# Moving one subtraction of DVE behind two maxima in a cross-attention and expert kernel

## The chip, the cores and the metric

The kernel runs on one core of a Trainium2 chip. The metric is the device time of one execution in microseconds (us). Engines are named as the profile names them: PE is TensorE's matmul, PEld its weight load, DVE is VectorE, ACT is ScalarE, POOL is GpSimd, SP issues DMAs.

## The reference

`x` has 16 batches of 224 tokens of width 512, the context 16 batches of 750 rows of width 384. All is float32.

```python
def _L0_xattn_ref(x, context, Wq, bq, Wk, bk, Wv, bv, Wo, bo):
    q = x @ Wq.T + bq
    k = context @ Wk.T + bk
    v = context @ Wv.T + bv
    ...                                   # 16 heads of 32
    attn = jnp.einsum('bihd,bjhd->bhij', q, k) * SCALE
    attn = jax.nn.softmax(attn, axis=-1)
    out = jnp.einsum('bhij,bjhd->bihd', attn, v)
    out = out.reshape(B, NQ, IN_DIM)
    return out @ Wo.T + bo
...
x = x + _L0_xattn_ref(_layernorm(x, axis=-1), ctx_768, ...)
x = x + _L0_ffn_ref(_layernorm(x, axis=-1), ...)   # 8 experts 512-256-512, GELU, top 2 by router logits
```

The router's logits of a token are its cosine with each expert's centroid plus its product with the expert's routing weights.

## The kernel before

The first four fifths of the time are attention, the last fifth the experts. Attention works on 64 groups `g`, four heads each, so a batch `b` has four groups, `t = g % 4`. Each engine has an order written out by hand: four functions `first`, `second`, `third` and `fourth`, one per group of a batch, called with `(g, g // 4)` for `g` from 0 to 68. Below, a "quarter" is one such call. The engines meet only through counting semaphores.

In the quarter of group `g`, TensorE computes the scores, exponentials' products with the values and denominators around group `g`, while it also makes the maxima's scores for group `g + 1` and the projected keys of group `g + 2` (`K0`, `K1`: the first 376 and the last 374 of them). Projections are made in float32 accuracy from two parts: ScalarE writes the high part of an operand (a rounded float32), and DVE the low part, which is the value less the high part. TensorE multiplies high by high, high by low and low by high (`split3`, lines 388 to 390).

- `maximum(g, m)`, DVE, m = 0 to 5: the row maxima of the scores of group `g`. TensorE writes those scores (`score_for_max`, line 1823) in three rounds, each into banks 0 to 3, and the next round, or another unit in one of these banks, waits until they have been reduced.
- `k_lo(g, i)`, DVE: the low part of the keys, after ScalarE's `k_hi`; it frees the bank of `K0` or `K1`.
- `o_lo(g)`, DVE, line 1291: the low part `oT_l` of the turned (transposed) and normalised outputs of group `g`. Both its inputs, `o_s` and `oT_h`, are in SBUF, as is its output. It waits for ScalarE's `o_hi(g)`. TensorE's `project_o` of the second quarter needs it for all four groups of a batch, and ScalarE's `o_copy` of the next group waits for it before it overwrites `o_s`.
- `keep_logits(b, qt)`, DVE, lines 1369 and 1371: copies the router logits of a batch from PSUM and adds the cosines. TensorE's `turn_logits` (line 1757) makes them. The second call frees the logits' bank.
- `add_step(g, i)`, POOL, lines 631 and 634: adds up exponentials of 125 x 896 columns for the denominators, five steps per group. In the first quarter `add_bo` (line 650) stands ahead of steps 1 to 4; it waits for the load of the residual `x_res`.

PSUM banks of the array `M` are handed out by a fixed plan (`bank_plan`). Around the boundary between the first and the second quarter bank 4 goes, in this order, to `lg` (the logits), `K0` of the second quarter and `xT0`. `K1` of the second quarter goes to bank 1. A unit in bank 1 waits for the last round of maxima scores that was planned ahead of it, here `maximum(g + 1, 2)` of the second quarter.

On TensorE the second quarter begins with `score_for_max(g + 1, 0)`, two scores, `project_k(g + 2, 0)` (K0), two scores, `score_for_max(g + 1, 1)`, `values(g - 1, 2)`, `transpose_x(b + 1, 0)`, two scores, `project_k(g + 2, 1)` (K1).

Of the kernel before, what the change touches and what calls it, by code (L numbers as in the profile page):

```python
# [12 lines left out]
B, NQ, D = 16, 224, 512  # L13
# [133 lines left out]
def expert_phase(nc, x1_d, w1, b1, w2, b2, centroids, w_route, ident_d, gates_dram, out):  # L147
    x, ctxT, wqT, bq, wkT, bk, wvT, bv, woT, bo, ident, x1 = SCRATCH["attention"]
    with ExitStack() as es:
# [209 lines left out]
        def bank_of(kind, n):  # L359
            return M[:, UNITS[kind, n][0], :]  # L360
# [9 lines left out]
        def freed(kind, n):  # L370
            return misc_free[UNITS[kind, n][0]]
# [28 lines left out]
        with nc.Block() as block:  # L400
# [794 lines left out]
            def _(dve):  # L1195
# [28 lines left out]
                def xT_rest(b, i):  # L1224
                    if b >= B:
                        return
                    dve.wait_ge(xT_hi, 2 * b + i + 1)
                    dve.tensor_tensor(out=xT_l[:, 2 * i:2 * i + 2, :],
                                      in0=bank_of(f"xT{i}", b)[:, 0:2 * NQ].rearrange("p (c n) -> p c n", c=2),
                                      in1=xT_h[:, 2 * i:2 * i + 2, :], op=ALU.subtract).then_inc(freed(f"xT{i}", b), 1)  # L1230

                def q_lo(g):
                    if g >= GROUPS:
                        return
                    dve.wait_ge(qh_done, g + 1)
                    dve.scalar_tensor_tensor(out=ql_s[:, g % 2, :], in0=bank_of("Q", g)[:, 0:NQ],
                                             scalar=bq_s[:, g % NG:g % NG + 1], in1=qh_s[:, g % 2, :], op0=ALU.add,
                                             op1=ALU.subtract).then_inc(freed("Q", g), 1)

                def k_lo(g, i):  # L1240
                    if g >= GROUPS:
                        return
                    off, w = KHALF[i]
                    dve.wait_ge(kh_done, 2 * g + i + 1)
                    dve.scalar_tensor_tensor(out=kl_s[:, g % 2, off:off + w], in0=bank_of(f"K{i}", g)[:, 0:w],  # L1245
                                             scalar=bk_s[:, g % NG:g % NG + 1], in1=kh_s[:, g % 2, off:off + w],
                                             op0=ALU.add, op1=ALU.subtract).then_inc(freed(f"K{i}", g), 1)

                def maximum(g, m):
                    if not 0 <= g < GROUPS:  # L1250
                        return
                    u, pair = m // 2, slice(m % 2 * 2, m % 2 * 2 + 2)
                    if m == 0 and g:
                        dve.wait_ge(top_done, g)
                    dve.wait_ge(x_full, XU * g + u + 1)
                    if u < QT:
                        dve.tensor_reduce(mx_parts[0:QP, pair, u, 0:1], M[0:QP, pair, 0:FIRST_KEYS], AX.X,  # L1257
                                          ALU.max).then_inc(max_done, 1)
                        return
                    both = M[0:QP, pair, 0:QT * OTHER_KEYS].rearrange("p j (q n) -> p j q n", q=QT)  # L1260
                    dve.tensor_reduce(mx_parts[0:QP, pair, :, 1], both, AX.X, ALU.max).then_inc(max_done, 1)  # L1261

                def top(g):
                    if not 0 <= g < GROUPS:
                        return
                    if g:
                        wait_full(dve, "mT", g - 1)
                    dve.wait_ge(max_done, 2 * XU * (g + 1))
                    dve.tensor_reduce(mx[0:QP, :], mx_parts[0:QP].rearrange("p j q k -> p (j q) k"), AX.X,
                                      ALU.max).then_inc(top_done, 1)  # L1270

                def invert(g):
                    if not 0 <= g < GROUPS:
                        return
                    wait_full(dve, "den", g)
                    den = bank_of("den", g)[:, 0:NQ]
                    dve.reciprocal(den, den).then_inc(inverted, 1)  # L1277

                def normalise(g):
                    if not 0 <= g < GROUPS:  # L1280
                        return
                    dve.wait_ge(inverted, g + 1)
                    dve.wait_ge(ocopy_done, g + 1)
                    dve.tensor_tensor(out=o_s[:, :], in0=o_s[:, :], in1=bank_of("den", g)[:, 0:NQ],
                                      op=ALU.mult).then_inc(freed("den", g), 1)

                def o_lo(g):
                    if not 0 <= g < GROUPS:
                        return
                    dve.wait_ge(oh_done, g + 1)  # L1290
                    dve.scalar_tensor_tensor(out=oT_l[:, g % OS, :], in0=o_s[:, :], scalar=bv_s[:, g % NG:g % NG + 1],
                                             in1=oT_h[:, g % OS, :], op0=ALU.add, op1=ALU.subtract).then_inc(ol_done, 1)

                def residual(b, qt):
                    if not 0 <= b < B:
                        return
                    wait_full(dve, f"O{qt}", b)
                    dve.wait_ge(bo_added, QT * b + qt + 1)
                    x = residual_of(b)[0:QP, qt, :]
                    dve.tensor_tensor(out=x, in0=bank_of(f"O{qt}", b)[0:QP, :], in1=x,  # L1300
                                      op=ALU.add).then_inc(freed(f"O{qt}", b), 1)
# [17 lines left out]
                def y_stats_half(b, qt):  # L1319
                    if b:  # L1320
                        dve.wait_ge(newton2, roots(b))
                    wait_free(dve, f"O{qt}", b)
                    dve.bn_stats(stats2[0:QP, qt, :], residual_of(b)[0:QP, qt, :]).then_inc(y_stat, 1)
# [35 lines left out]
                def keep_logits(b, qt):  # L1359
                    if not 0 <= b < B:  # L1360
                        return
                    if b == B - 1:
                        last_logits(qt)
                        return
                    wait_full(dve, "lg", b)
                    dve.wait_ge(newton2, roots(b + 1))
                    both = logits_of(b, qt)
                    kept = lgs[0:QP, QT * b + qt, :]
                    dve.tensor_copy(kept, both[:, E:2 * E]).then_inc(lg_copied, 1)
                    dve.wait_ge(lg_copied, 3 * b + 2 * qt + 1)  # L1370
                    dve.scalar_tensor_tensor(out=kept, in0=both[:, 0:E], scalar=length[0:QP, qt:qt + 1], in1=kept,  # L1371
                                             op0=ALU.mult, op1=ALU.add).then_inc(freed("lg", b) if qt else lg_copied, 1)
# [24 lines left out]
                def w_part(n):  # L1397
                    src, hi, lo = pieces[n]
                    dve.wait_ge(ew_hi, n + 1)
                    dve.tensor_tensor(out=lo, in0=lo.bitcast(F32), in1=hi, op=ALU.subtract).then_inc(ew_lo, 1)  # L1400
# [14 lines left out]
                def first(g, b):  # L1415
                    maximum(g + 1, 0)
                    maximum(g + 1, 1)
                    k_lo(g + 2, 0)
                    q_lo(g + 2)
                    maximum(g + 1, 2)  # L1420
                    invert(g - 1)
                    maximum(g + 1, 3)
                    normalise(g - 1)
                    k_lo(g + 2, 1)
                    maximum(g + 1, 4)
                    maximum(g + 1, 5)
                    top(g + 1)
                    q_lo(g + 3)
                    o_lo(g - 1)
                    keep_logits(b - 2, 0)  # L1430
                    keep_logits(b - 2, 1)

                def second(g, b):
                    maximum(g + 1, 0)
                    maximum(g + 1, 1)
                    k_lo(g + 2, 0)
                    maximum(g + 1, 2)
                    xT_rest(b + 1, 0)
                    maximum(g + 1, 3)
                    invert(g - 1)  # L1440
                    k_lo(g + 2, 1)
                    normalise(g - 1)
                    residual(b - 1, 0)
                    if b == B:
                        y_stats_half(B - 1, 0)
                        w_part(4)
                    maximum(g + 1, 4)
                    maximum(g + 1, 5)
                    xT_rest(b + 1, 1)
                    top(g + 1)  # L1450
                    residual(b - 1, 1)
# [755 lines left out]
```

## Time and profile before

| | |
|---|---|
| median of three timed runs | 1476.07 us (1475.44 to 1480.64) |
| the profiled execution | 1481.48 us |
| its span in the profile | 1479.7 us |
| TensorE busy | 1393.8 us, 94% |
| POOL busy | 1078.5 us, 73% |
| DVE busy | 987.6 us, 67% |
| ScalarE busy | 840.7 us, 57% |

The span is what the profiler's records cover; the profiled execution's own time is 1.8 us more. Busy shares are averages over stages; which engine sets the time at a place is read from what waits for what there. Records of one engine can overlap by some 0.09 us, and an instruction's record can hold time in which it is held up. The rows that are used stand in their own section below.

### The profile page before, as it was taken

Reading aid. Unit: us, or ns where it says so; the run is one execution under the profiler, and the core shown is the slowest. Engines: PE = TensorE matmul, PEld = TensorE weight load, DVE = VectorE, ACT = ScalarE, POOL = GpSimd, SP = SyncE. Lnnn points to the kernel's source line nnn. Section 1 sums busy time; section 2 is a strip of 40 time slices with the busy share of each in tenths; the row PEclk is TensorE's granted clock in tenths of the full one; section 3 lists DMA queues with packets and bytes.
Section 4 is the critical chain, followed back from the end, with each engine's and each line's share of the span. In section 5 each row is a group of like instructions: output and inputs, shape, how many; then the busy total and the mean of one; then the engine's idle time right before and its main releaser. Section 6 shows DMA issues by size and latency. Waiting matters only on the chain.

```text
span 1479.7 us, 34315 instructions
## 1 busy us (share of the span) xinstructions
PE 1393.8 (94%) x11524; PEld 1110.1 (75%) x11524; DVE 987.6 (67%) x1429; ACT 840.7 (57%) x1825; POOL 1078.5 (73%) x915
## 2 busy tenths in 40 slices
PE   4899999999999999999999999999998777999997
PEld 4677777777777777778777777777786446888896
DVE  6666777767676767777777776767667485444443
ACT  4556655556656565666665555555564553555554
POOL 3468787877787878787877878777877814666765
PEclk9989999999999999999999999999999687999999
DMA  7354555555455554555555454545444753777775
GB/s 244 89 133 109 160 141 141 148 131 147 125 154 138 146 139 133 141 142 140 152 138 165 122 161 130 145 131 149 113 132 125 235 130 83 141 139 131 143 140 83
DMA packets 134952, 206.74 MB, mean 140 GB/s; under 512 B 33808, under 2 KB 70832, under 8 KB 134656
## 3 DMA queue, kind: packets, MB, share of 16 engines
q1 hardware_dynamic: 120544, 173.20, 43.2%
q0 software_dynamic: 14240, 31.35, 11.9%
q8 instruction: 99, 1.62, 0.5%
q14 instruction: 69, 0.57, 0.1%
HBM read 64.29 MB, written 38.66 MB: 70 GB/s over the span
## 4 chain that ended last, share of the span: by engine, by line
PE 83%; DVE 8%; SPq 3%; issue 2%; DMA 1%; ACT 1%; POOL 1%; POOLq 0%; DVEq 0%; ACTq 0%
PE M L388 14%; PE M L389 12%; PE M L390 12%; PE S L1846 11%; PE O L1862 9%; PE M L1823 5%; DVE mx_parts L1261 2%; PE M L2119 2%; PE M L2118 2%; PE M L2117 2%; PE M L2136 2%; PE M L2137 2%; PE M L2138 2%; PE S L2107 2%; PE M L1880 2%
## 5 line engine op out<-in xcount | busy, mean ns | idle before, releaser
L634 POOL TENSOR_TENSOR psum_p<-psum_p,pr 125x896 f32<-125x896 f32 x254 | 542.7, 2137 | 109.7 <-ACT pr L917 84.3
L917 ACT ACTIVATE pr<-S 125x448 f32<-125x448 f32 x768 | 386.8, 542 | 204.4 <-PE S L1846 198.4
L1257 DVE TENSOR_REDUCE mx_parts<-M 112x2 f32<-112x1024 f32 x256 | 305.7, 1216 | 83.7 <-PE M L1823 83.6
L1846 PE MATMUL S<-qst,kst 128*125 128x224 f32 x1536 | 268.7, 289 | 6.3 <-ACT pr L917 2.6
L1846 PEld LDWEIGHTS S<-qst,kst 128*125 128x125 f32 x1536 | 224.1, 190 | 54.9 <-issue 22.8
L1862 PE MATMUL O<-pr,v 125*32 125x224 f32 x3072 | 183.9, 361 | 0.1
L1261 DVE TENSOR_REDUCE mx_parts<-M 112x4 f32<-112x952 f32 x128 | 140.9, 1143 | 59.0 <-PE M L1823 58.9
L631 POOL TENSOR_TENSOR psum_p<-pr 125x896 f32<-125x896 f32 x64 | 135.2, 2113 | 48.7 <-ACT pr L917 48.5
L388 PE MATMUL M<-ctx_h,wk_h 128*128 128x376 f32 (+1 forms) x384 | 137.3, 358 | 7.5 <-DVE lgs L1371 6.7
L885 ACT ACTIVATE kh_s<-M,bk_s 128x376 fp32r<-128x376 f32 (+1 forms) x128 | 73.1, 571 | 109.9 <-PE M L390 107.0
L389 PE MATMUL M<-ctx_l,wk_h 128*128 128x376 f32 (+1 forms) x384 | 130.1, 339 | 0.0
L390 PE MATMUL M<-ctx_h,wk_l 128*128 128x376 f32 (+1 forms) x384 | 129.5, 337 | 0.0
L809 POOL DMA_INDIRECT out<-y_out,table_t x63 | 99.9, 1585 | 40.2 <-ACT y_out L1177 20.0
L1862 PEld LDWEIGHTS O<-pr,v 125*32 125x32 f32 x3072 | 85.9, 110 | 53.0 <-issue 14.0
L1277 DVE RECIPROCAL M<-M 128x224 f32<-128x224 f32 x64 | 100.1, 1564 | 37.8 <-PE M L1880 37.6
L801 POOL DMA_INDIRECT xg<-rows_d,table_x x63 | 64.0, 1016 | 83.9 <-DVE settled L1657 40.7
L388 PE MATMUL M<-wv_h,ctx_h 128*125 128x512 f32 x288 | 117.0, 406 | 0.2 <-DVE wv_l L1198 0.2
L390 PE MATMUL M<-wv_h,ctx_l 128*125 128x512 f32 x288 | 113.6, 394 | 0.0
L389 PE MATMUL M<-wv_l,ctx_h 128*125 128x512 f32 x288 | 113.4, 394 | 0.0
L1823 PE MATMUL M<-kh_s,q_own 32*112 32x512 f32 (+1 forms) x1024 | 94.5, 400 | 16.6 <-DVE mx_parts L1257 7.5
L1245 DVE SCALAR_TENSOR_TENSOR kl_s<-M,bk_s,kh_s 128x376 fp32r<-128x376 f32 (+1 forms) x128 | 76.6, 598 | 22.3 <-ACT kh_s L885 22.0
L388 PEld LDWEIGHTS M<-ctx_h,wk_h 128*128 128x128 f32 x384 | 73.5, 191 | 22.0 <-issue 12.5
(259 smaller groups left out, 2985.1 us busy)
## 6 DMA issues: line engine op xcount, KB each, us to landing
kst<-kh_s SPq DMA_DIRECT2D x512, 93.8 KB, 2.2
kst<-kl_s SPq DMA_DIRECT2D x256, 93.8 KB, 2.2
ctx_r<-ctxT SPq DMA_DIRECT2D x48, 375.0 KB, 3.9
qst<-qh_s SPq DMA_DIRECT2D x128, 112.0 KB, 2.9
rows_d<-x_res SPq DMA_DIRECT2D x32, 448.0 KB, 5.0
w_l<-w SPq DMA_DIRECT2D x16, 512.0 KB, 7.8
x_ln<-x SPq DMA_DIRECT2D x17, 448.0 KB, 4.7
q_own<-qh_s SPq DMA_DIRECT2D x256, 28.0 KB, 1.8
```

Source lines behind the costliest of these rows:

```text
L388: pe.matmul(out, lhs[0], rhs[0], start=first, stop=False)
L389: pe.matmul(out, lhs[0], rhs[1], start=False, stop=False)
L390: return pe.matmul(out, lhs[1], rhs[0], start=False, stop=last)
L631: pool.tensor_tensor(out=total, in0=tiles[0], in1=tiles[1], op=ALU.add).then_inc(sum_step, 1)
L634: pool.tensor_tensor(out=total, in0=total, in1=tiles[half], op=ALU.add).then_inc(sum_step, 1)
L917: act.activation(pr[0:KP, (3 * g + p) % 2, j, :, :], S[0:KP, n % SB, 0:2 * NQ].rearrange("p (i n) -> p i n", i=2), ACT.Exp).then_inc(exp_d ...
L1257: dve.tensor_reduce(mx_parts[0:QP, pair, u, 0:1], M[0:QP, pair, 0:FIRST_KEYS], AX.X, ALU.max).then_inc(max_done, 1)
L1261: dve.tensor_reduce(mx_parts[0:QP, pair, :, 1], both, AX.X, ALU.max).then_inc(max_done, 1)
L1277: dve.reciprocal(den, den).then_inc(inverted, 1)
L1823: last = pe.matmul(M[0:QP, j, at:at + w], q_own[head, g % 2, QP * qt:QP * (qt + 1)], kh_s[head, g % 2, off:off + w], start=True, stop=True)
L1846: last = pe.matmul(S[0:KP, n % SB, NQ * h:NQ * (h + 1)], kst[:, i, j, o:o + KP], qst[:, i, j, :], start=True, stop=True)
L1862: last = pe.matmul(O[HD * j:HD * (j + 1), 0:NQ], v[0:KP, 2 * p + i, HD * j:HD * (j + 1)], pr[0:KP, (3 * g + p) % 2, j, i, :], start=(p == ...
```

## The change

In the first quarter `o_lo(g - 1)`, the low part of the last group of the batch before, no longer stands ahead of the two `keep_logits`; only in the round after the last batch (b == B, B is 16) it keeps its place. For the batches 1 to 15 it is issued in the second quarter, as `o_lo(g - 2)`, behind `maximum(g + 1, 0)` and `maximum(g + 1, 1)` and ahead of `k_lo(g + 2, 0)`. (At b = 0 there is no such group, and the call returns.)

```diff
@@ -1426,13 +1426,16 @@
                     maximum(g + 1, 5)
                     top(g + 1)
                     q_lo(g + 3)
-                    o_lo(g - 1)
+                    if b == B:
+                        o_lo(g - 1)
                     keep_logits(b - 2, 0)
                     keep_logits(b - 2, 1)
 
                 def second(g, b):
                     maximum(g + 1, 0)
                     maximum(g + 1, 1)
+                    if b < B:
+                        o_lo(g - 2)
                     k_lo(g + 2, 0)
                     maximum(g + 1, 2)
                     xT_rest(b + 1, 0)
```

## Rows read from the trace of the kernel before

**Rows 1.** The page: span and busy time of each engine.

```profile
span 1479.7 us, 34315 instructions
...
PE 1393.8 (94%) x11524; PEld 1110.1 (75%) x11524; DVE 987.6 (67%) x1429; ACT 840.7 (57%) x1825; POOL 1078.5 (73%) x915
```

**Rows 2.** Busy time by stretch, cut at the start of each first-quarter L1291.

```profile
core 0: us, PE busy (x) PEld busy (x) DVE busy (x) ACT busy (x) POOL busy (x), PEclk, DMA share, GB/s
...
694.76:764.32 69.56, 69.17 (x616) 54.37 (x616) 50.09 (x71) 42.54 (x96) 55.77 (x50) 1.00 0.53 144
...
834.65:905.95 71.30, 69.39 (x616) 54.42 (x616) 51.88 (x72) 42.54 (x96) 56.95 (x50) 1.00 0.53 141
```

**Rows 3.** Timeline around one cut: start us, us, instruction, idle before and releaser.

```profile
623.88 2.09 POOL L634 TENSOR_TENSOR psum_p<-psum_p,pr 125x896 f32<-125x896 f32 x1
...
626.11 2.11 POOL L634 TENSOR_TENSOR psum_p<-psum_p,pr 125x896 f32<-125x896 f32 x1
...
628.36 2.10 POOL L634 TENSOR_TENSOR psum_p<-psum_p,pr 125x896 f32<-125x896 f32 x1
...
624.88 1.34 DVE L1291 SCALAR_TENSOR_TENSOR oT_l<-o_s,bv_s,oT_h 128x224 fp32r<-128x224 f32 x1
...
625.28 0.47 PE L1757 MATMUL M<-pick,lg_parts 128*112 128x16 f32 x4
...
626.14 0.15 DVE L1369 COPY lgs<-M 112x8 f32<-112x8 f32 x1
...
626.80 2.35 DVE L1257 TENSOR_REDUCE mx_parts<-M 112x2 f32<-112x1024 f32 x2
...
626.94 0.44 PE L388 MATMUL M<-ctx_h,wk_h 128*128 128x376 f32 x1
...
629.48 0.61 DVE L1245 SCALAR_TENSOR_TENSOR kl_s<-M,bk_s,kh_s 128x376 fp32r<-128x376 f32 x1 [0.33 <-ACT kh_s L885]
...
630.01 1.22 DVE L1257 TENSOR_REDUCE mx_parts<-M 112x2 f32<-112x1024 f32 x1
...
631.49 0.34 PE L388 MATMUL M<-ctx_h,wk_h 128*128 128x374 f32 x1
...
631.75 0.35 ACT L927 ACTIVATE o_s<-O 128x224 f32<-128x224 f32 x1
```

**Rows 4.** Who waited for the kept logits: us, times.

```profile
PEld M L388: 10.3, 13
```

**Rows 5.** Timeline, two races of L1291 with an add of POOL.

```profile
593.54 0.44 DVE L1291 SCALAR_TENSOR_TENSOR oT_l<-o_s,bv_s,oT_h 128x224 fp32r<-128x224 f32 x1
...
593.71 2.24 POOL L634 TENSOR_TENSOR psum_p<-psum_p,pr 125x896 f32<-125x896 f32 x1 [0.43 <-POOL psum_p L634]
...
905.95 2.43 DVE L1291 SCALAR_TENSOR_TENSOR oT_l<-o_s,bv_s,oT_h 128x224 fp32r<-128x224 f32 x1
...
906.03 2.10 POOL L634 TENSOR_TENSOR psum_p<-psum_p,pr 125x896 f32<-125x896 f32 x1
```

**Rows 6.** Timeline, a cut where POOL's four adds start early.

```profile
693.45 8.88 POOL L634 TENSOR_TENSOR psum_p<-psum_p,pr 125x896 f32<-125x896 f32 x4
...
694.76 1.04 DVE L1291 SCALAR_TENSOR_TENSOR oT_l<-o_s,bv_s,oT_h 128x224 fp32r<-128x224 f32 x1
...
695.72 0.15 DVE L1369 COPY lgs<-M 112x8 f32<-112x8 f32 x1
...
696.58 0.39 PE L388 MATMUL M<-ctx_h,wk_h 128*128 128x376 f32 x1
...
701.08 0.34 PE L388 MATMUL M<-ctx_h,wk_h 128*128 128x374 f32 x1
```

**Rows 7.** Timeline, the cut where they start latest.

```profile
834.65 2.83 DVE L1291 SCALAR_TENSOR_TENSOR oT_l<-o_s,bv_s,oT_h 128x224 fp32r<-128x224 f32 x1
...
835.14 8.84 POOL L634 TENSOR_TENSOR psum_p<-psum_p,pr 125x896 f32<-125x896 f32 x4
...
838.21 0.44 PE L388 MATMUL M<-ctx_h,wk_h 128*128 128x376 f32 x1 [1.57 <-DVE lgs L1371]
...
842.76 0.34 PE L388 MATMUL M<-ctx_h,wk_h 128*128 128x374 f32 x1
```

**Rows 8.** Timeline, third maximum of a second quarter, and K1.

```profile
1125.64 2.35 DVE L1257 TENSOR_REDUCE mx_parts<-M 112x2 f32<-112x1024 f32 x2
...
1127.01 0.41 PE L388 MATMUL M<-ctx_h,wk_h 128*128 128x374 f32 x1
```

## The prediction

> **What bounds the kernel now.** I read the page first: TensorE is busy for 94% of the span, DVE for 67%, POOL for 73% [rows 1]. So only what makes TensorE wait counts. Next the table by stage, cut at the last-group low part of each batch (L1291 in the first quarter): between two such cuts TensorE has 69.1 to 69.7 us of work in thirteen of fourteen stretches, and the length of the stretch is that work plus its stalls: 69.56 us for one without a stall at the cut, 71.30 us for one that has one [rows 2]. A stall is not made good within the batch; it is passed on whole.
>
> Then the timeline around one cut, batch 9 to 10. "K0" is the first matmul of the first half of the next keys in the second quarter, "K1" that of the second half. K0 writes the bank that held the logits, so it waits for the second `keep_logits`. On DVE the low part stands ahead of both `keep_logits`; it was dispatched at 624.88 and ended at 626.22, the logits' matmul started at 625.28 and took 0.47, the first copy of the logits began at 626.14, the maxima at 626.80, and K0 at 626.94 [rows 3]. The list of who waits for the kept logits puts 10.3 us in 13 waits on TensorE's weight loads [rows 4].
>
> **Why the low part is long.** Where nothing is in its way it takes 0.44 us [rows 5]; here it took 1.34. POOL's add of 896 columns ran from 623.88 to 625.97, and the low part ended 0.25 after it [rows 3]. In the fifteen cuts (batches 1 to 15) it always ended 0.24 to 0.27 us after the end of one of POOL's four adds, and lasted from 1.04 [rows 6] to 2.83 us [rows 7]. So an add in progress holds it up till the add's end. The maxima (each 1.2 us with or without an add beside them) are not held up. Call T the low part's start and p the start of POOL's first add less T: p is -1.31 in the case of rows 6, +0.49 in that of rows 7, -1.00 in rows 3. Over the fifteen cuts p is -1.31 three times, -1.22, -1.04, -1.00, -0.97, -0.84, then -0.56, -0.55, -0.49, then -0.20, +0.08, +0.09, +0.49.
>
> **What the change takes away.** With the low part gone, the copy can begin when the logits are there, at T+0.96 as in rows 6, where K0 starts at T+1.82 (696.58 less 694.76). Batch 1, which keeps no logits, also has K0 at T+1.82, so TensorE is ready no earlier. The gain at K0 is its start less (T+1.82): 626.94 gives 0.24 in rows 3, 838.21 gives 1.74 in rows 7, 0 in rows 6. The other twelve cuts give, worked out alike, 0, 0.28, 0.70, 0.21, 0, 0.12, 0.43, 0.76, 1.34, 1.36, 1.06, 0.69: together 8.9 us. That is all the change can give.
>
> **What it puts in.** The maxima now start at T+1.64 and last 2.35 (with 0.09 of overlap, as all rows of DVE overlap), so the low part is dispatched at T+3.90. Behind it on DVE stand `k_lo(g + 2, 0)` (0.61 us) and `maximum(g + 1, 2)` (1.22), and K1 needs the latter, since it writes a bank that this maximum reads. Before, `k_lo` waits for ScalarE and starts 2.5 us after K0 (629.48), the maximum at 630.01 ends at 631.23, and K1 starts at 631.49, 4.55 after K0 [rows 3]. The least distance from that maximum's end to K1 is seen where TensorE does wait for it: 1125.64 plus 1.22 to 1127.01, 0.15 us [rows 8]. So the slack before K1 is 0.26 less 0.15: 0.1 us. With an unheld 0.44 the low part ends at T+4.34, `k_lo` would start at T+4.32 anyway, and it is free. But POOL's adds follow each other 2.24 us apart and last 2.10 [rows 3]: the third runs from p+4.48 to p+6.58. With p under -0.46 the second has ended before T+3.90 and the low part meets the third: it ends at p+6.83, `k_lo` starts 0.08 earlier, and K1 comes 1.89 us after `k_lo`'s start (0.53 and 1.22 and 0.14), at p+8.64. With p above -0.46 it waits for the second add only and K1 is at p+6.40, but not before T+6.32.
>
> Against the old K1 at each cut: rows 6, 693.45+8.64 = 702.09 against 701.08, 1.01 us later; rows 3, 632.52 against 631.49, 1.03 later. All eleven cuts with p at -0.49 or under come out 0.99 to 1.17 later, 11.4 us together, whatever they had lost at K0, because both waits end with an add of the same chain, two adds apart. The four late ones gain: rows 7, 835.14+6.40 = 841.54 against 842.76, 1.22; the others 1.23, 1.23 and 1.10, 4.8 us together. Sum: +6.6 us, on the profiled execution's 1481.48.
>
> Three cuts (p -0.56, -0.55, -0.49) are near the edge: at T+3.90 the second add has ended and the third's record starts 0.02, 0.03 and 0.09 us later. I read the race from rows: dispatched 0.08 ahead of the add, the low part lost it and lasted 2.43; 0.17 ahead it won and lasted 0.44, the add 2.24 [rows 5]. So I count the three as lost. If all were won they would gain 0.6 to 0.8 each in place of losing 1.0, and the sum would be +1.4.
>
> The Trainium skill ("SBUF — State Buffer", Who interferes with whom) says that a DVE instruction with two SBUF inputs and a GpSimd instruction that reads SBUF exclude each other for the whole instruction, and that whoever starts first goes on. The trace agrees with the blocking; taken at its word for recorded starts, the rule would let the low part win at the three cuts and give +1.4 us, where the row with a lead of 0.08 gives +6.6. The measurement decides for me.
>
> The rest costs nothing. The number of instructions is unchanged. Nothing moves on the DMA queues. `o_copy` in the second quarter waits for the low part, but it starts at T+6.87 (631.75) [rows 3], later than p+6.83 for every early cut. `project_o` reads the result later still. In the last round (b = 16) the order stays as it was.
>
> **From the profiled execution to the median.** The three timed runs have a median 5.4 us under the profiled 1481.48. p depends on when the residual load lands, and a late landing is also what makes the old waits at K0 long; quicker runs probably had fewer. With thirteen early and two late cuts the sum would be 13.3 - 2.4 = +10.9. I take a value between that and +6.6: +8.7, so 1484.8 us.
>
> **Rivals.** (a) The wait is nearly always there: all fifteen cuts early, +15.5 us, 1491.6. For it: eleven are early here and every early one costs the same. Against: four were late in this execution. (b) The other side: POOL's chain starts after T-0.46 at all cuts, the low part ends with the second add or finds none, and only the gain at K0 is left. This execution's 8.9 us give 1467.2, the timed ones, with fewer waits to remove, up to 1472. It decides at p = -0.46, so the residual load would have to land 0.1 to 0.85 us later than in the eleven early cuts. Against: three cuts sit at -1.31, the value of batch 1, where no load is waited for. (c) The stall at K1 is made good: were TensorE to wait after it for something not tied to it, the loss goes and so does the gain; 1476, give or take 3. Against: rows 2 show whole stalls passed on, 1.74 us against 71.30 less 69.56.
>
> **Numbers.** Forecast as summed, 0.54; (a) 0.15; (b) 0.12; (c) 0.19. The likeliest case by itself reaches from 1478 (the three edge cuts won) to 1488. The range, 1472 to 1491, takes in (c), nearly all of (a) and the slow end of (b). A change within 0.5% (7.4 us) can't be told from none: that bound, 1483.5, cuts the forecast; I give some 0.37 of its 0.54 to slower, the rest to same. Slower 0.37 + 0.14 = 0.51; same 0.17 + 0.01 + 0.19 = 0.37; faster 0.12, from (b).
>
> **What would show it.** In the profile after, the copy of the logits starts near T+0.96 with no L1291 before it and K0 near T+1.82 in every batch, T now being the end of the `q_lo` in front. The moved L1291 lasts 0.4 to 2.6 us and ends 0.25 after an add of POOL. TensorE's waits for the kept logits go, and in their place its L388 waits for the maxima (L1257), about 1 us at some eleven cuts. Wrong if the moved L1291 stays at 0.44, or if it is long and K1 does not move; the size is wrong if p is distributed otherwise.

## The result, and the profile after

The changed kernel's median is 1464.02 us (1461.1 to 1467.88, 6 runs) against 1474.99 us of the kernel before in 6 runs. The ratio is 0.993, with a 95% interval of 0.9911 to 0.9948. That is 11 us faster, beyond the 0.5% that a measurement here can tell from nothing. 1484.8 us and a range of 1472 to 1491 us were forecast.

The profiled execution took 1467.88 us. Its page, span and busy time (to [rows 1]):

```profile
span 1466.0 us, 34315 instructions
...
PE 1389.4 (95%) x11524; PEld 1109.4 (76%) x11524; DVE 970.8 (66%) x1429; ACT 840.8 (57%) x1825; POOL 1082.7 (74%) x915
```

DVE is 17 us less busy, POOL 4 us more. Who waited for the kept logits in the kernel after (to [rows 4]); the one wait left belongs to the last round:

```profile
PEld M L388: 0.9, 1
```

The timeline of the kernel after around the cut of batch 2 (to [rows 3, 6]; the columns are start, duration, instruction):

```profile
202.67 0.17 DVE L1369 COPY lgs<-M 112x8 f32<-112x8 f32 x1 [0.84 <-PE M L1760]
...
203.56 0.36 PE L388 MATMUL M<-ctx_h,wk_h 128*128 128x376 f32 x1
...
202.71 2.11 POOL L634 TENSOR_TENSOR psum_p<-psum_p,pr 125x896 f32<-125x896 f32 x1
...
204.96 3.05 POOL L634 TENSOR_TENSOR psum_p<-psum_p,pr 125x896 f32<-125x896 f32 x1
...
204.47 1.22 DVE L1257 TENSOR_REDUCE mx_parts<-M 112x2 f32<-112x1024 f32 x1
...
205.60 0.44 DVE L1291 SCALAR_TENSOR_TENSOR oT_l<-o_s,bv_s,oT_h 128x224 fp32r<-128x224 f32 x1
...
206.01 0.61 DVE L1245 SCALAR_TENSOR_TENSOR kl_s<-M,bk_s,kh_s 128x376 fp32r<-128x376 f32 x1
206.54 1.22 DVE L1257 TENSOR_REDUCE mx_parts<-M 112x2 f32<-112x1024 f32 x1
208.04 0.34 PE L388 MATMUL M<-ctx_h,wk_h 128*128 128x374 f32 x1
```

T is 201.75 here (`q_lo` began at 201.39, and what stands behind it starts 0.36 later). The copy starts at T+0.92 and K0 at T+1.81, as forecast. The low part is dispatched at T+3.85, 0.64 us into POOL's third add, again as forecast. But it takes 0.44 us, and it is the add that is held: 3.05 us in place of 2.11. K1 starts 4.48 us after K0, without a wait; at thirteen of the fifteen cuts this distance is 4.33 to 4.53 us.

The low part lasts 0.44 us at 14 of the 15 cuts. At twelve of them its dispatch falls between 0.12 us before and 0.66 us after the start of an add, and that add lasts 2.28 to 3.07 us; at the other two it falls in the last 0.2 us of one and ends 0.25 us after it. POOL's phase is spread as before: its first add starts 1.31 to 0.54 us before T at eleven cuts, later at four. The exception, in the timeline of the kernel after:

```profile
904.01 2.10 POOL L634 TENSOR_TENSOR psum_p<-psum_p,pr 125x896 f32<-125x896 f32 x1
...
905.18 1.18 DVE L1291 SCALAR_TENSOR_TENSOR oT_l<-o_s,bv_s,oT_h 128x224 fp32r<-128x224 f32 x1
...
908.15 0.41 PE L388 MATMUL M<-ctx_h,wk_h 128*128 128x374 f32 x1 [0.17 <-DVE mx_parts L1257]
```

Here the second add began 1.17 us ahead of the low part, a little before the maximum in front of it (904.05), and the low part ended 0.25 us after that add. K1 came 0.5 us late. (The other cut with a late K1 is the one where POOL's adds start latest; see below.)

The busy time by stretch, K0 to K0, of the kernel after (to [rows 2]; the first column is the length): all batches from 1 to 15, one ordinary one, and the one with the latest residual load.

```profile
134.01:1112.37 978.36, 969.93 (x8598) 762.07 (x8597) 693.10 (x976) 594.47 (x1343) 794.63 (x679) 1.00 0.53 142
...
623.12:692.63 69.51, 69.16 (x616) 54.42 (x615) 49.55 (x71) 42.54 (x97) 56.62 (x49) 1.00 0.53 144
831.69:903.13 71.44, 69.92 (x616) 54.49 (x615) 49.53 (x71) 42.54 (x97) 58.01 (x50) 1.00 0.53 140
```

The same fourteen batches took 989.08 us in the kernel before (133.51 to 1122.59, K0 to K0): 10.7 us more. A batch without a stall is 69.5 us in both.

### The profile page after: what moved, and what is told of

Same layout as the page of the kernel before. It is cut to its first block, busy times and chain, and to the rows that moved or that the text cites. A ratio compares the mean times of both kernels' runs of the same rounds, so it can differ in the third digit from the quotient of the medians.

```text
span 1466.0 us, 34315 instructions
## 1 busy us (share of the span) xinstructions
PE 1389.4 (95%) x11524; PEld 1109.4 (76%) x11524; DVE 970.8 (66%) x1429; ACT 840.8 (57%) x1825; POOL 1082.7 (74%) x915
## 4 chain that ended last, share of the span: by engine, by line
PE 87%; DVE 5%; POOL 2%; issue 2%; DMA 2%; SPq 1%; ACT 1%; POOLq 0%; DVEq 0%; ACTq 0%
PE M L388 13%; PE S L1849 12%; PE M L389 12%; PE M L390 12%; PE O L1865 10%; PE M L1826 5%; PE M L2122 2%; PE M L2121 2%; PE M L2120 2%; PE M L2139 2%; PE M L2140 2%; PE M L2141 2%; PE S L2110 2%; PE M L1883 2%; POOL psum_p L634 1%
## 5 line engine op out<-in xcount | busy, mean ns | idle before, releaser
L634 POOL TENSOR_TENSOR psum_p<-psum_p,pr 125x896 f32<-125x896 f32 x254 | 549.8, 2165 | 107.5 <-ACT pr L917 82.1
L388 PE MATMUL M<-ctx_h,wk_h 128*128 128x376 f32 (+1 forms) x384 | 136.2, 355 | 0.6 <-DVE mx_parts L1257 0.5
L809 POOL DMA_INDIRECT out<-y_out,table_t x63 | 99.9, 1585 | 39.0 <-ACT y_out L1177 17.9
L388 PE MATMUL M<-wv_h,ctx_h 128*125 128x512 f32 x288 | 117.1, 407 | 0.0
L1826 PEld LDWEIGHTS M<-kh_s,q_own 32*112 32x112 f32 x1024 | 41.8, 170 | 62.3 <-issue 48.1
L1245 DVE SCALAR_TENSOR_TENSOR kl_s<-M,bk_s,kh_s 128x376 fp32r<-128x376 f32 (+1 forms) x128 | 76.5, 598 | 16.2 <-ACT kh_s L885 15.8
```

The lines of the kernel that those rows point to most:

```text
L388: pe.matmul(out, lhs[0], rhs[0], start=first, stop=False)
L634: pool.tensor_tensor(out=total, in0=total, in1=tiles[half], op=ALU.add).then_inc(sum_step, 1)
L1826: last = pe.matmul(M[0:QP, j, at:at + w], q_own[head, g % 2, QP * qt:QP * (qt + 1)], kh_s[head, g % 2, off:off + w], start=True, stop=True)
```

## The experiments

Each ratio is to the kernel before, run beside it on the same chip. T and p are the prediction's: T is when the low part would be dispatched in its old place, p is the start of POOL's first add less T. The edits of runs 1 to 4, 7, 8 and 10 are told against the changed kernel, those of runs 5, 6 and 9 against the kernel before. Where fourteen cuts are counted, that of batch 1, which keeps no logits, is left out.

"The port" stands below for whatever the low part and an add of POOL can't use at the same time. The traces show only that one of the two is held while the other runs. An add or a low part "wins" when it takes its usual time (2.1 and 0.44 us), and "loses" when it is held by the other. A "seam" is the place where one instruction of POOL ends and the next begins.

**1. A short instruction between the second maximum and the low part.**

```diff
+                def short():
+                    dve.tensor_reduce(settled[:, :], ones[:, 0:2], AX.X, ALU.max)
...
                     maximum(g + 1, 1)
-                    if b < B:
+                    if 1 <= b < B:
+                        short()
                         o_lo(g - 2)
```

> The changed kernel with one short reduction on DVE (two columns, SBUF to SBUF, some 0.1 to 0.2 us, its value the same constant) put between the second maximum and the moved low part, for the batches 1 to 15. Theory A: DVE asks for the read port that it shares with POOL for its next instruction with two SBUF inputs as soon as the instruction before it runs. Behind a maximum of 1.2 us that is early enough to get the port in the gap behind POOL's second add; behind the short reduction it is not, and the low part meets the third add at the early cuts (some 11 of 15), lasts 1 to 2.6 us there, and TensorE's K1 is 1.0 to 1.7 us late: 12 to 16 us slower than the changed kernel, so a ratio to the kernel before of 1.000 to 1.006. Theory B: it is the place, or the phase against POOL's adds, that keeps the low part free, not what runs right before it. Then the low part keeps 0.44 us and the ratio is 0.992 to 0.995.

Ratio 1.0017 (1.0001 to 1.0033), median 1477.57 us. Its timeline at the cut of batch 3:

```profile
273.34 2.35 DVE L1257 TENSOR_REDUCE mx_parts<-M 112x2 f32<-112x1024 f32 x2
...
275.60 0.15 DVE L1435 TENSOR_REDUCE settled<-ones 128x1 f32<-128x2 f32 x1
275.67 2.25 DVE L1291 SCALAR_TENSOR_TENSOR oT_l<-o_s,bv_s,oT_h 128x224 fp32r<-128x224 f32 x1
...
279.71 0.41 PE L388 MATMUL M<-ctx_h,wk_h 128*128 128x374 f32 x1 [0.18 <-DVE mx_parts L1257]
...
275.58 2.09 POOL L634 TENSOR_TENSOR psum_p<-psum_p,pr 125x896 f32<-125x896 f32 x1
```

With 0.15 us of other work in front of it, the low part is dispatched 0.09 us after the third add's start and loses to it; 0.64 us after, but right behind a maximum, it had won. It lasts 1.4 to 2.3 us at 10 of 14 cuts. The transposes behind `k_lo` wait 10.0 us in ten waits, and L388 another 3.7 for the maxima. Here K1 starts at T+7.97 with p at -0.68, so at p+8.65, where the prediction had worked out p+8.64. That is the slow-down that it had forecast for the change itself.

**2. The control: the short instruction ahead of the second maximum.**

```diff
                     maximum(g + 1, 0)
+                    if 1 <= b < B:
+                        short()
                     maximum(g + 1, 1)
```

> The control for the run with the short reduction between: the same short reduction stands ahead of the second maximum, so the low part still follows a maximum directly. Both theories: the low part lasts 0.44 us at nearly all cuts, and the kernel is at most 1.5 us slower than the changed one, ratio to before 0.992 to 0.996. If this one is slow too, the short reduction itself has a price and the other run says nothing.

Ratio 0.9939 (0.992 to 0.9959), median 1465.79 us. At its first cut:

```profile
203.08 1.22 DVE L1257 TENSOR_REDUCE mx_parts<-M 112x2 f32<-112x1024 f32 x1
...
204.21 0.44 DVE L1291 SCALAR_TENSOR_TENSOR oT_l<-o_s,bv_s,oT_h 128x224 fp32r<-128x224 f32 x1
...
203.77 2.85 POOL L634 TENSOR_TENSOR psum_p<-psum_p,pr 125x896 f32<-125x896 f32 x1
```

The same instructions and the same place of the low part to within 0.1 us; only what runs right before it differs. It lasts 0.44 or 0.45 us at 12 of 14 cuts, and the kernel is 11.8 us faster than that of run 1.

**3. Only one part of the change: the low part behind the kept logits, ahead of the maxima.**

```diff
                     keep_logits(b - 2, 1)
+                    if b < B:
+                        o_lo(g - 1)
 ...
                     maximum(g + 1, 1)
-                    if b < B:
-                        o_lo(g - 2)
```

> One part of the change alone: the low part goes behind the two keep_logits but stays ahead of the maxima. Theory A: it asks for the port at about T+1.45, during the last short step of keep_logits. Where POOL's chain starts at T-0.93 or earlier, the second add has the port, the low part ends 0.25 us after that add (T+3.3 to 3.7), the maxima and with them TensorE's second round of maxima scores are 1.7 to 2 us late; at the other cuts it costs 0.3 to 1.3. Sum 13 to 17 us on top of the changed kernel, ratio to before 1.001 to 1.006. Theory B (it is enough to have it out of the way of keep_logits): 0.44 us in front of the maxima, of which 0.15 is slack, 4 to 5 us over the changed kernel, ratio 0.995 to 0.997.

Ratio 1.0067 (1.0048 to 1.0087), median 1485.69 us, a little over what theory A gave. Its timeline at the cut of batch 3:

```profile
273.41 0.23 DVE L1371 SCALAR_TENSOR_TENSOR lgs<-M,length,lgs 112x8 f32<-112x8 f32 x1
273.55 2.26 DVE L1291 SCALAR_TENSOR_TENSOR oT_l<-o_s,bv_s,oT_h 128x224 fp32r<-128x224 f32 x1
275.73 2.35 DVE L1257 TENSOR_REDUCE mx_parts<-M 112x2 f32<-112x1024 f32 x2
...
278.22 0.50 PE L1826 MATMUL M<-kh_s,q_own 32*112 32x512 f32 x4 [2.30 <-DVE mx_parts L1257]
...
273.44 2.12 POOL L634 TENSOR_TENSOR psum_p<-psum_p,pr 125x896 f32<-125x896 f32 x1
```

Behind a step of 0.23 us the low part loses to an add that began 0.11 us earlier. Clearing it out of the way of the logits alone is no gain: the wait of K0 goes, and the second round of maxima scores waits 2.3 us instead.

**4. Behind one maximum.** `o_lo(g - 2)` between the two maxima.

> The changed kernel with the low part behind the first maximum of the second quarter in place of the second. Theory A: it asks at about T+1.8; where POOL's chain starts before T-0.6 the second add has the port by then, the low part lasts 0.5 to 1.3 us and the second maximum ends 0.3 to 1.0 us too late for TensorE; elsewhere it takes the port, 0.44 us, 0.2 us late. 5 to 9 us over the changed kernel, ratio to before 0.996 to 0.999. Theory C (an instruction behind a maximum is never held up, whatever POOL does): 0.44 us everywhere, 3 to 4 us over the changed kernel, ratio 0.995 to 0.996.

Ratio 0.9997 (0.998 to 1.0013), median 1473.39 us: the low part lasts 0.54 to 1.02 us at eight cuts and 0.44 at six. Theory C (behind a maximum the low part is never held) is out. TensorE's waits of line 1826 for the maxima are 17.9 us in 19 waits against 7.7 in 4 of the changed kernel, and the kernel is 9.4 us slower than that one, just above theory A's range.

**5. POOL's four adds split, without a gap.** In the kernel before, the adds of 896 columns at a cut become two of 448, the second without a wait.

```diff
+                        if g % NG == 0 and 0 < g < GROUPS - NG + 1:
+                            first, rest = slice(0, GH // 2), slice(GH // 2, GH)
+                            add = pool.tensor_tensor(out=total[:, first, :], in0=total[:, first, :],
+                                                     in1=tiles[half][:, first, :], op=ALU.add)
+                            pool.tensor_tensor(out=total[:, rest, :], in0=total[:, rest, :],
+                                               in1=tiles[half][:, rest, :], op=ALU.add).then_inc(sum_step, 1)
+                            return
```

> The kernel before, with each of POOL's four adds at a cut (batches 1 to 15) split into two of 448 columns, the second right behind the first with no semaphore between. It tells who gets the port when POOL has its next instruction ready at once. Theory D (taken from the late cuts of the kernel before, where the low part lost the port to the first add that followed the residual's addition without a gap): POOL keeps the port through both halves, the low part still ends with a whole add, lasts 1.0 to 2.8 us, and the waits for the kept logits stay at 6 to 12 us; ratio 0.999 to 1.003. Rival E (any end of an instruction of POOL lets DVE in): the low part ends 0.25 us after a half, at most 1.5 us long, the waits for the logits fall to under 3 us, and the ratio is 0.994 to 0.997.

Ratio 0.9993 (0.9977 to 1.0009), median 1474.7 us. Its timeline at one cut (the low part is L1298 in this kernel):

```profile
624.46 1.15 POOL L636 TENSOR_TENSOR psum_p<-psum_p,pr 125x448 f32<-125x448 f32 x1
...
625.57 1.14 POOL L638 TENSOR_TENSOR psum_p<-psum_p,pr 125x448 f32<-125x448 f32 x1
...
625.64 1.31 DVE L1298 SCALAR_TENSOR_TENSOR oT_l<-o_s,bv_s,oT_h 128x224 fp32r<-128x224 f32 x1
```

It ends 0.24 us after the second half. At another cut it was dispatched at 765.33, a first half ended at 766.15, the second half ran to 767.25, and the low part ended at 767.50: it was there 0.8 us before the seam and was not let in. Nine times in this run a seam fell while the low part waited. At seven of them POOL kept the port; at two, 486.27 and this one, it did not, although the code is the same:

```profile
906.58 1.14 POOL L636 TENSOR_TENSOR psum_p<-psum_p,pr 125x448 f32<-125x448 f32 x1
906.68 1.28 DVE L1298 SCALAR_TENSOR_TENSOR oT_l<-o_s,bv_s,oT_h 128x224 fp32r<-128x224 f32 x1
907.68 1.29 POOL L638 TENSOR_TENSOR psum_p<-psum_p,pr 125x448 f32<-125x448 f32 x1
```

So theory D holds for the time and for most seams, but it is no rule. In the traces of runs 9 and 10 a low part of a later quarter waits over the seam between the last add of one group and the first of the next 26 times, there is no gap either, and it is let in each time. What decides at a seam without a gap is not shown.

**6. The same with a gap.** The second half waits for a semaphore that the first sets.

```diff
+                            add.then_inc(half_sum, 1)
+                            pool.wait_ge(half_sum, 4 * (g // NG - 1) + i)
```

> The same as the split run, but the second half waits for a semaphore that the first half sets, which makes a gap of some 0.13 us. Both theories: DVE gets in at the half. The low part lasts at most 1.5 us at nearly all cuts, the waits for the kept logits fall from 8.9 to under 3 us, ratio 0.993 to 0.997, if POOL's extra 0.2 to 0.3 us per add (4 adds, 15 batches) is hidden; where it is not, ScalarE waits for POOL's sums and up to 5 us of it come back. If the low part is as long as before, the holding by POOL's add is not what makes it long.

Ratio 0.9978 (0.9966 to 0.9989), median 1471.73 us. Its timeline at the same cut as above (L1301 is the low part):

```profile
623.43 1.15 POOL L637 TENSOR_TENSOR psum_p<-psum_p,pr 125x448 f32<-125x448 f32 x1
...
623.95 0.88 DVE L1301 SCALAR_TENSOR_TENSOR oT_l<-o_s,bv_s,oT_h 128x224 fp32r<-128x224 f32 x1
```

It ends 0.25 us after the first half. With the gap of 0.08 us the low part is let in at all nine seams that fall while it waits. At fourteen cuts it lasts 0.44 to 1.31 us, where run 5 had 0.87 to 2.21, and of TensorE's waits for the logits at the cuts only 0.2 us at each of two cuts is left. Less than the whole gain arrives, and the ratio is a little above the forecast 0.993 to 0.997: ScalarE now waits 15.8 us in nine waits for POOL's sums, which take longer.

**7. Behind the third maximum.** `o_lo(g - 2)` after `maximum(g + 1, 2)`, so that nothing that K1 needs is queued behind it.

> The changed kernel with the low part behind the third maximum of the second quarter, so that neither the keys' low part nor the maximum that K1 needs is queued behind it. Theory A: it asks while that maximum runs (T+4.8 on) and meets the third or the gap before the fourth add, lasts 0.4 to 0.9 us, is done by T+6.4, before ScalarE's copy needs it at T+6.9; nothing is queued behind it that TensorE waits for. As fast as the changed kernel or up to 2 us faster: ratio 0.991 to 0.994. Rival: the low part is late for ScalarE's copy, and values and scores follow late: ratio 0.994 to 0.998.

Ratio 0.9946 (0.9925 to 0.9966), median 1467.87 us. The low part lasts 0.44 to 0.46 us at twelve of fourteen cuts. The ratio lies in the range of the rival, not in theory A's, but the interval reaches into both and overlaps that of the change: whether this place is as good is open, and it is not shown to be better.

**8. Behind the keys' low part.** `o_lo(g - 2)` between `k_lo(g + 2, 0)` and `maximum(g + 1, 2)`.

> The changed kernel with the low part behind k_lo(g + 2, 0), ahead of the third maximum. Theory A: k_lo starts at T+4.3 only, so the port is asked for when POOL's third add has it at every cut with p under -0.3. The low part ends at p+6.8, lasts 0.7 to 1.8 us, and K1 is 0.4 to 1.2 us late there: 8 to 12 us over the changed kernel, ratio 0.998 to 1.001. Theory B (the place behind the maxima is free whatever runs in between): 0.44 us, 4 to 5 us over the changed kernel, ratio 0.995 to 0.997.

Ratio 1.0048 (1.0029 to 1.0067), median 1481.67 us. Its waits on TensorE (us, times, longest), and one cut in its timeline:

```profile
PE M L388 <- DVE mx_parts L1257: 13.3, 14, 1.6
```

```profile
276.94 0.61 DVE L1245 SCALAR_TENSOR_TENSOR kl_s<-M,bk_s,kh_s 128x376 fp32r<-128x376 f32 x1 [0.32 <-ACT kh_s L885]
277.47 1.03 DVE L1291 SCALAR_TENSOR_TENSOR oT_l<-o_s,bv_s,oT_h 128x224 fp32r<-128x224 f32 x1
...
279.78 0.41 PE L388 MATMUL M<-ctx_h,wk_h 128*128 128x374 f32 x1 [0.65 <-DVE mx_parts L1257]
```

The low part is held at 12 of 14 cuts (0.85 to 2.02 us). One step further down the queue than in the change, the low part turns a gain of 11 us into a loss of 7. Theory A gave 8 to 12 us over the changed kernel, and it is 17.6. The waits of K1 make 13.3 of them; where the rest comes from is open.

**9 and 10. The residual's bias addition behind the four adds**, in the kernel before (9) and in the changed one (10). POOL's adds then start with ScalarE's exponentials, not with a load.

```diff
                     add_step(g, 0)
-                    if b < B:
-                        add_bo(b - 1)
                     add_step(g, 1)
 ...
                     add_step(g, 4)
+                    if b < B:
+                        add_bo(b - 1)
```

> The kernel before, with POOL's addition of the output bias to the residual (which waits for a DMA) moved from ahead of the four adds at a cut to behind them. The adds then start when ScalarE's exponentials allow it, not when a load lands. If the old waits for the kept logits come from where POOL's adds stand against the low part, p is -1.3 at every cut, the low part lasts 1.04 us each time, and those waits fall from 7.6 us to under 1. POOL reaches the second quarter up to 2 us later than in an early cut, so the time may keep a part of the 8.9 us: ratio 0.993 to 0.999. If the waits come from something else, they stay.

Ratio 0.9941 (0.9921 to 0.9961), median 1464.56 us. A cut in its timeline:

```profile
688.45 2.11 POOL L634 TENSOR_TENSOR psum_p<-psum_p,pr 125x896 f32<-125x896 f32 x1 [5.67 <-ACT pr L917]
...
689.75 1.05 DVE L1291 SCALAR_TENSOR_TENSOR oT_l<-o_s,bv_s,oT_h 128x224 fp32r<-128x224 f32 x1
...
691.58 0.40 PE L388 MATMUL M<-ctx_h,wk_h 128*128 128x376 f32 x1
```

p is -1.30 or -1.31 at thirteen of fourteen cuts, the low part lasts 1.04 to 1.06 us there, and K0 is at T+1.81 to T+1.83. The low part is in its old place, and the kernel is as fast as the changed one. So the time that the change wins is indeed the wait of K0, and that wait comes from the phase of POOL's adds.

> The changed kernel with the same move of the bias addition. Every cut should be like the early cuts of the changed kernel: the low part lasts 0.44 us and stretches POOL's third add by 0.9; no low part near 1.2 us, no wait of ScalarE for POOL of 2 us as at the latest cut. If POOL's later start of the second quarter is hidden, it is 0 to 3 us faster than the changed kernel, ratio 0.990 to 0.993; if not, ScalarE and TensorE wait for POOL's sums and the ratio is 0.994 to 0.999.

Ratio 1.0008 (0.9993 to 1.0024), median 1474.05 us: slower than either edit alone, outside both forecasts. The low part lasts 0.44 us at every cut, but POOL, with the bias addition behind it, now pays for it: ScalarE waits 8.2 us in nine waits for POOL's sums (0.9 us in one wait in run 9), the scores wait 6.3 us for the maxima's DMA, and the second round of maxima scores 11.7 us in 16 waits against 7.7 in 4. Whether these waits make up the 9.5 us between runs 9 and 10 is open.

## Why the prediction was wrong

The step that failed is "With p under -0.46 the second has ended before T+3.90 and the low part meets the third: it ends at p+6.83". It took the low part's claim on the port to begin with its dispatch, and so K1 to come about 1.0 us later at eleven cuts, 11.4 us together. In its place the low part took 0.44 us there, the third add was held instead (to 3.05 us in the lines above), and K1 did not move. The wait of K0 that went, 8.9 us by the prediction's own sum, was a gain with nothing against it.

Runs 1 and 2 show that what runs right before the low part decides: behind a maximum of 1.2 us it wins against an add that starts up to 0.66 us before its dispatch, behind 0.15 us of other work it loses to one that starts 0.09 us before. The traces of all runs narrow it down. This is the closest loss behind a maximum, in run 2's timeline:

```profile
831.44 1.22 DVE L1257 TENSOR_REDUCE mx_parts<-M 112x2 f32<-112x1024 f32 x1
831.47 2.11 POOL L634 TENSOR_TENSOR psum_p<-psum_p,pr 125x896 f32<-125x896 f32 x1
832.57 1.25 DVE L1291 SCALAR_TENSOR_TENSOR oT_l<-o_s,bv_s,oT_h 128x224 fp32r<-128x224 f32 x1
```

And this is the closest win, in run 7's:

```profile
978.41 1.22 DVE L1257 TENSOR_REDUCE mx_parts<-M 112x2 f32<-112x1024 f32 x1
978.50 3.48 POOL L634 TENSOR_TENSOR psum_p<-psum_p,pr 125x896 f32<-125x896 f32 x1
979.54 0.45 DVE L1291 SCALAR_TENSOR_TENSOR oT_l<-o_s,bv_s,oT_h 128x224 fp32r<-128x224 f32 x1
```

The add that held the low part began 0.03 us after the start of the maximum ahead of it. The add that was held itself (3.48 us) began 0.09 us after that start, and still a microsecond before the low part's own record. A border of the same kind shows behind the two shorter steps. Behind the 0.15 us of run 1 the low part loses to an add that began 0.01 us after that step did (346.87) and wins against one 0.08 us after (1054.16). Behind the 0.23 us of run 3 it loses at 0.03 (273.55) and wins at 0.18 us (345.81). The twelve traces hold some 440 low parts right behind a reduction or behind one of these steps that met an add which followed a gap, at the cuts and elsewhere, and none of them breaks this. So the start of the add is to be compared with the start of the instruction ahead, not with that of the low part. Length alone is not all of it: behind `k_lo`, 0.61 us long (run 8), the low part still loses to an add that began 0.20 us after `k_lo` did (703.97) and wins at 0.61 us (916.52).

The reading that fits is that DVE claims the port for its next instruction when the one before starts; then the claim stands when the second add ends, and the third waits. That the claim is made so early is inferred from who wins; no record shows it.

The trace of the kernel before had this race already. In the third quarter of each of the first fifteen batches another low part stands right behind a maximum. Fourteen of these were dispatched 0.12 to 0.47 us after an add had begun, and all of them won; the fifteenth is the one that won in rows 5. One of them in the timeline of the kernel before:

```profile
238.45 1.23 DVE L1257 TENSOR_REDUCE mx_parts<-M 112x2 f32<-112x1024 f32 x1 [1.85 <-PE M L1823]
239.47 2.52 POOL L634 TENSOR_TENSOR psum_p<-psum_p,pr 125x896 f32<-125x896 f32 x1
239.59 0.44 DVE L1291 SCALAR_TENSOR_TENSOR oT_l<-o_s,bv_s,oT_h 128x224 fp32r<-128x224 f32 x1
```

These were the rows to read the new place from. The prediction took its lost race from the old place [rows 5].

- What bounds the kernel, K0 at T+1.82 (T+1.60 at one cut), a saving of the whole wait there, and stalls passed on whole: right. The price of the wait was 8.9 us by the sum and 10.7 between the two profiled executions from batch 1 to batch 15; 11 in the medians. (One of the twelve small gains, 0.12 us, is 0.04 by the rule that the prediction gives, at the cut of 485.00; the sum stays 8.9 to within 0.1.) Most of the other 1.8 us is one stretch of the old execution in which TensorE's granted clock was 0.50, the lower of its two levels, for some 3.4 us from 980.46 on, so that its work took 70.90 us in place of 69.3 to 69.7. In the new execution every stretch from K0 to K0 has 1.00. The busy time by stretch of the kernel before:

```profile
980.28:1052.30 72.02, 70.90 (x615) 55.95 (x615) 51.20 (x71) 42.54 (x96) 56.53 (x50) 0.98 0.52 139
982.00:983.00 1.00, 1.00 (x5) 1.00 (x4) 0.48 (x1) 0.00 (x0) 1.00 (x1) 0.50 0.34 116
```

  The clock fell right behind the wait of K0 at that cut (TensorE had 0.08 us of work from 979.00 to 980.20), but the longer wait of rows 7 had no such fall behind it. That the wait caused it is not shown.
- "That is all the change can give": right in kind, 2 us small against the medians, inside their interval (8 to 13 us).
- The dispatch at T+3.90, the third maximum of the quarter as what K1 waits for, K1 at 1.89 us after `k_lo`: right (1.87 us in run 1, 277.84 to 279.71). In run 1 the early cuts cost about what the sum said: it is 13.6 us slower than the changed kernel, where +6.6 against a full gain of 8.9 makes 15.5.
- The race: the row where the low part was dispatched 0.08 us ahead of the add and lost [rows 5] was read as the rule for all. There the add followed POOL's bias addition without a gap, while the third add follows the second with one of 0.14 us. Run 6 shows what the gap does behind the same `q_lo` (0.44 us long), in its timeline:

```profile
554.13 0.44 DVE L1301 SCALAR_TENSOR_TENSOR oT_l<-o_s,bv_s,oT_h 128x224 fp32r<-128x224 f32 x1
554.16 1.41 POOL L641 TENSOR_TENSOR psum_p<-psum_p,pr 125x448 f32<-125x448 f32 x1
```

  With a gap of 0.08 us a lead of 0.03 us was enough. The other difference between the row and the new place is what ran ahead, `q_lo` and not a maximum.
- The rule of the Trainium skill that I set against it ("SBUF — State Buffer", Who interferes with whom: whoever issues first holds the pair for its whole instruction) was nearer: the traces agree that one excludes the other for a whole instruction, 2.10 us and 0.44 us. The prediction took the recorded start for the issue, which gives +1.4 us and not -11: the holder is not the one whose record starts first. If issue is the moment of the claim, the runs put it near the start of the instruction ahead.
- Rival (b) had the right outcome, that only the gain at K0 is left, with 1467.2 to 1472 us for it; 1464.02 is 3 us under that. It had the wrong condition: p did not move, eleven cuts are still under -0.46. It was given 0.12.
- "Each 1.2 us with or without an add beside them" held for the maxima, but the low part's own price is not gone, only moved: POOL is held for 0.2 to 1.0 us at twelve cuts, 5.3 us of busy time over the fourteen batches. The hold is hidden, save at the latest cut (831.69 to 903.13), where POOL's adds start at p = +0.98, one is stretched to 3.04 us and ScalarE waits 2.11 us for the sum; that batch is the one of 71.44 us.

## What to carry to other kernels

When two engines exclude each other, work out for each placement who claims first, and count the instruction ahead in the queue as part of the claim: behind a reduction the low part won when that reduction had started before POOL's add did, by 0.1 us or more, so a long one ahead let DVE win the next seam and a short one let it lose. Look in the trace for the same instruction in the same company (what runs ahead of it, what gap the rival has) before a race is read from another place. Then ask whether the engine that now waits has slack, for the hold does not go away, it changes sides. And look at what sets the phase between them: here a load that lands early or late decided a wait of TensorE, and taking the load out of POOL's way gave the same 0.6% as moving the instruction.

## What the hardware showed that was not expected

- A DVE instruction with two SBUF inputs was held to the end of POOL's add (0.24 to 0.27 us after it) or went through in 0.44 us and stretched the add by its place in it plus 0.3 us (0.64 us in, 0.94 us longer), as though the add, already recorded as begun, had not got its data.
- Behind a maximum, the low part won against adds that began up to 1.04 us before its dispatch (979.54, run 7) and lost to one that began 1.10 us before (832.57, run 2). The border lies 0.03 to 0.09 us after the start of the maximum; behind steps of 0.15 and 0.23 us it lies at 0.01 to 0.08 and 0.03 to 0.18 us after their start.
- At a seam of POOL with a gap of 0.08 us, made by a semaphore, the waiting low part got in nine times out of nine (run 6, 623.95). At the same seams without a gap it was kept out seven times of nine (run 5: 2.17 us at 765.33, let in at 906.68).
